# Embedding bags by counting: VectorE parts four table chunks instead of three, and ScalarE copies every upper part

## The reference, cut to what matters

```python
flat = tables.reshape(F_ * V_, E_)
emb = flat[ids + offs]                      # 512 x 32 x 20 x 64
mask = (jnp.arange(L_) < lengths[..., None]).astype(emb.dtype)
pooled = jnp.einsum('bfle,bfl->bfe', emb, mask)
return jnp.nan_to_num(pooled.reshape(Bq, F_ * E_))
```

## Time and profile before

| | |
|---|---|
| time, median of 3 runs | 1303.89 us (1300.76 to 1318.76) |
| the profiled execution's own time | 1306.5 us |
| its span | 1304.4 us |
| mean granted clock of TensorE | 0.934 |
| busy share of the span | PE 77%, DVE 71%, ACT 62%, POOL 55% |
| chain of work that ended last, by engine | PE 55%, ACT 18%, DVE 11%, another core or an unknown queue 8%, issue 7% |

### The profile page before, as it was taken

How to read it: one execution, slowest core, us unless ns; L and a number is a source line. 1 busy time by engine, 2 the same in 40 slices (tenths; PEclk the granted TensorE clock), 3 DMA queues, 4 the chain that set the end, 5 groups by cost and what they waited for, 6 DMA issues and landing times.

```text
span 1304.4 us, 28164 instructions
## 1 busy us (share of the span) xinstructions
PE 1002.7 (77%) x9391; PEld 835.3 (64%) x9391; DVE 929.9 (71%) x2543; ACT 811.9 (62%) x1198; POOL 721.5 (55%) x667
## 2 busy tenths in 40 slices
PE   3438887886887787778788777787878778879996
PEld 1226776765766666566666566675767666767876
DVE  9915757785977776767777677786777768768891
ACT  3525857674857575657475656675767666667881
POOL 3874656665665565645756646666666665652010
PEclk9958999998989988989989899998999989899998
DMA  4402322433333423224242424251515242413120
GB/s 176 168 10 56 79 73 64 120 99 96 105 102 100 122 79 114 84 63 129 79 120 77 123 60 128 72 157 43 149 52 156 65 127 74 124 35 106 45 66 6
DMA packets 67286, 120.72 MB, mean 93 GB/s; under 512 B 32329, under 2 KB 34131, under 8 KB 67208
## 3 DMA queue, kind: packets, MB, share of 16 engines
q1 hardware_dynamic: 45240, 99.89, 24.2%
q0 software_dynamic: 20768, 19.49, 7.8%
q10 hardware_dynamic: 1200, 0.62, 0.2%
HBM read 81.61 MB, written 4.75 MB: 66 GB/s over the span
## 4 chain that ended last, share of the span: by engine, by line
PE 55%; ACT 18%; DVE 11%; another core or an unknown queue 8%; issue 7%; DVEq 0%; DMA 0%
PE sums L575 30%; PE pairs L566 19%; ACT counts L508 10%; PE rest L594 5%; DVE onehot_j L792 4%; ACT rest L516 3%; ACT parts L525 2%; ACT parts L533 1%; DVE onehot_p L790 1%; ACT parts L529 1%; ACT parts L521 1%; DVE table L804 1%; DVE parts L810 1%; DVE rows L852 0%
## 5 line engine op out<-in xcount | busy, mean ns | idle before, releaser
L461 POOL DMA_INDIRECT rows<-tables,row_now x537 | 595.7, 1109 | 417.9 <-PE pairs L566 261.2
L575 PE MATMUL sums<-parts,counts 128*128 128x192 bf16 x7448 | 785.8, 255 | 0.8 <-issue 0.8
L508 ACT ACTIVATE counts<-pairs 128x588 int16<-128x588 f32 (+1 forms) x836 | 529.8, 649 | 392.1 <-PE pairs L566 255.4
L575 PEld LDWEIGHTS sums<-parts,counts 128*128 128x128 fp8e3 x7448 | 672.7, 102 | 51.6 <-issue 1.6
L566 PE MATMUL pairs<-onehot_j,onehot_p 128*128 128x294 bf16 x1634 | 366.5, 306 | 177.9 <-ACT counts L508 116.5
L792 DVE TENSOR_SCALAR onehot_j<-ramp,j_of,worth 128x296 bf16<-128x296 f16 x1596 | 470.1, 356 | 0.0
L790 DVE TENSOR_TENSOR onehot_p<-ramp,p_of 128x768 bf16<-128x768 f16 x266 | 146.6, 551 | 329.1 <-PE pairs L566 226.4
L566 PEld LDWEIGHTS pairs<-onehot_j,onehot_p 128*128 128x128 bf16 x1634 | 158.2, 101 | 263.8 <-issue 168.1
L471 POOL DMA_INDIRECT out_gathered<-gathered,place_now x52 | 59.7, 1147 | 99.0 <-DVE gathered L822 83.7
L525 ACT ACTIVATE parts<-rest 128x896 bf16<-128x896 f32 x76 | 69.6, 916 | 40.9 <-remote 24.7
L594 PE MATMUL rest<-table,minus_eye 128*128 128x448 bf16 x152 | 46.4, 388 | 51.4 <-ACT rest L516 33.7
(11 more groups left out here) (74 smaller groups left out, 238.0 us busy)
## 6 DMA issues: line engine op xcount, KB each, us to landing
table<-tables SPq DMA_DIRECT2D x133, 448.0 KB
rows<-zeros SPq DMA_DIRECT2D x52, 640.0 KB
rows<-tables,row_now POOLq DMA_INDIRECT x537
out_counted<-pooled SPq DMA_DIRECT2D x114, 21.0 KB
sorted_records<-records,rank POOLq DMA_INDIRECT x52
out_gathered<-gathered,place_now POOLq DMA_INDIRECT x52
rows<-lookup_ids SPq DMA_DIRECT2D x1, 774.0 KB, 7.9
rows<-lookup_lengths SPq DMA_DIRECT2D x1, 774.0 KB, 9.2
```

What stands on the lines that cost most here:

```text
L461: nc.gpsimd.indirect_dma_start(out=rows[:, k, l * E:(l + 1) * E], out_offset=None, in_=table_rows, in_offset=bass.IndirectOffsetOnAxis(ap= ...
L508: nc.scalar.activation(dst, src, ACT.Copy).then_inc(counts_saved, 1)
L575: last = nc.tensor.matmul(sums[h][:, k * PARTS * E:(k + 1) * PARTS * E], counts[h][:, j, :, k], parts[:, j].rearrange("p t e -> p (t e)"), ...
```

## The change

VectorE parts chunk 4 as well, so it has chunks 1, 3, 4 and 6, and PE's way is left with 0, 2 and 5. ACT copies the upper halves of all seven chunks (`HIGH_AT` has seven entries), and DVE's clamp (`cut_high`) and its semaphore are gone. `cut_rest` subtracts the upper halves of the words, read in the chunk itself with a stride of two bfloat16, and writes the remainder into a new buffer `remains` that holds two chunks, in place of the chunk. `save_cut_middle` and `cut_low` read that buffer. In a first use of a chunk PE waits for its upper part too. Slots and stages of most of this work are moved.

```diff
-PARTED_AT = {0: 9, 2: 16, 4: 24, 5: 29}
-HIGH_AT = {0: 7, 2: 15, 4: 21, 5: 28}
-PARTED_BY_VECTOR = {5: 1, 8: 3, 11: 6}
-MIDDLE_AT = {1: 14, 3: 23, 6: 32}
-BF16_MAX = 3.3895313892515355e38
+PARTED_AT = {0: 9, 2: 16, 5: 28}
+HIGH_AT = {0: 7, 1: 12, 2: 19, 3: 22, 4: 24, 5: 25, 6: 34}
+PARTED_BY_VECTOR = {5: 1, 7: 3, 9: 4, 11: 6}
+MIDDLE_AT = {1: 14, 3: 20, 4: 26, 6: 32}
...
+        remains = sb("remains", [P, 2, CE], F32)
...
+        def remains_of(c):
+            return remains[:, by_vector.index(c) % 2, :].rearrange("p (j e) -> p j e", e=E)
...
             def save_cut_middle(f, c):
                 act.wait_ge(rest_done, f * len(by_vector) + by_vector.index(c) + 1)
-                nc.scalar.activation(part_rows(1, c), table_rows_of(c), ACT.Copy).then_inc(cut_middle_saved, 1)
+                nc.scalar.activation(part_rows(1, c), remains_of(c), ACT.Copy).then_inc(cut_middle_saved, 1)
...
                             if h == 1 and q == 0:
+                                pe.wait_ge(high_saved, f * CHUNKS + (c + 1))
                                 if c in PARTED_AT:
                                     pe.wait_ge(low_saved, parted(f, c))
...
-            def cut_high(f, c):
-                dve.wait_ge(table_in[c], f * 16 + 16)
-                nc.vector.tensor_scalar(part_rows(0, c), table_rows_of(c), BF16_MAX, -BF16_MAX, ALU.min,
-                                        ALU.max).then_inc(high_done, 1)
             def cut_rest(f, c):
-                dve.wait_ge(high_done, f * len(by_vector) + by_vector.index(c) + 1)
-                nc.vector.tensor_tensor(table_rows_of(c), table_rows_of(c), part_rows(0, c),
-                                        ALU.subtract).then_inc(rest_done, 1)
+                dve.wait_ge(table_in[c], f * 16 + 16)
+                uppers = whole(c).bitcast(BF16).rearrange("p (j e y) -> p j e y", e=E, y=2)[:, :, :, 1]
+                nc.vector.tensor_tensor(remains_of(c), table_rows_of(c), uppers, ALU.subtract).then_inc(rest_done, 1)
             def cut_low(f, c):
                 dve.wait_ge(cut_middle_saved, f * len(by_vector) + by_vector.index(c) + 1)
-                nc.vector.tensor_tensor(part_rows(2, c), table_rows_of(c), part_rows(1, c),
+                nc.vector.tensor_tensor(part_rows(2, c), remains_of(c), part_rows(1, c),
                                         ALU.subtract).then_inc(parts_ready, 1)
...
                     onehots(f, h, c, i)
-                    if stage in PARTED_BY_VECTOR and i == 0:
-                        cut_high(f, PARTED_BY_VECTOR[stage])
-                    if stage in PARTED_BY_VECTOR and i == 2:
+                    if stage in PARTED_BY_VECTOR and i == 1:
                         cut_rest(f, PARTED_BY_VECTOR[stage])
                     if stage - 1 in PARTED_BY_VECTOR and i == 4:
                         cut_low(f, PARTED_BY_VECTOR[stage - 1])
```

More of the change, by code:

```diff
@@ L120, in build_embedding_bag @@
     assert LAST_BODY in (SLOTS, BUFFERS) and BUFFERS % 2 == 0 and BODIES > 1
+    assert sorted(HIGH_AT) == sorted(HIGH_AT, key=HIGH_AT.get) == list(range(CHUNKS))
     assert J % CHUNKS == 0 and GROUPS * GROUP >= HALF and PER_CHUNK % 2 == 0 and CHUNKS * PER_CHUNK == LAST
@@ L234, in build_embedding_bag @@
         table_in = [sem(f"table_in{c}") for c in range(CHUNKS)]
-        high_done = sem("high_done")
         rest_done = sem("rest_done")
@@ L793, in onehots, with cut_rest @@
                                         ALU.is_equal, ALU.mult).then_inc(onehots_ready, 1)
-            def cut_high(f, c):
+            def cut_rest(f, c):
                 dve.wait_ge(table_in[c], f * 16 + 16)
-                nc.vector.tensor_scalar(part_rows(0, c), table_rows_of(c), BF16_MAX, -BF16_MAX, ALU.min,
-                                        ALU.max).then_inc(high_done, 1)
-            def cut_rest(f, c):
-                dve.wait_ge(high_done, f * len(by_vector) + by_vector.index(c) + 1)
-                nc.vector.tensor_tensor(table_rows_of(c), table_rows_of(c), part_rows(0, c),
-                                        ALU.subtract).then_inc(rest_done, 1)
+                uppers = whole(c).bitcast(BF16).rearrange("p (j e y) -> p j e y", e=E, y=2)[:, :, :, 1]
+                nc.vector.tensor_tensor(remains_of(c), table_rows_of(c), uppers, ALU.subtract).then_inc(rest_done, 1)
             def cut_low(f, c):
                 dve.wait_ge(cut_middle_saved, f * len(by_vector) + by_vector.index(c) + 1)
-                nc.vector.tensor_tensor(part_rows(2, c), table_rows_of(c), part_rows(1, c),
+                nc.vector.tensor_tensor(part_rows(2, c), remains_of(c), part_rows(1, c),
                                         ALU.subtract).then_inc(parts_ready, 1)
```

## The result

In the first series the kernel before took 1314.94 us (median of five runs, the three shown and two new ones, 1300.76 to 1318.76) and the changed kernel 1293.44 us (1287.75 to 1308.06). The ratio is 0.987, with a 95% interval from 0.982 to 0.991: 1.3% faster, where 2.1% was forecast. The profiled execution of the changed kernel was the slowest of its five, 1308 us against 1288 to 1294, so its span is not compared with that of before; its slots are.

The account below looks back on a forecast made before the run. PE was taken as the bound, DVE right behind. Terms -1.95 - 0.6 + 0.6 + 0.4 = -1.55 us a field, over 18 fields 28 us: 1306.5 to 1278.5, less 2.6 for the median, 1276 us; range 1256 to 1308.

Parts of the forecast that it names:

- within 2%: Outcome class for the whole time, neither faster than 1278 us nor slower than 1330 us: chance 0.48.
- late results: PE results coming late in fields other than 17, costing 10 to 14 us a field; the prediction held them fixed.
- ACT's queue: One more ACT operation a field, lag in slots 16 to 26: +0.6 us, the middle of nothing to 1.2.
- the cuts beside the gathers: Two more long DVE cuts a field beside POOL's gathers: at most 2.2 us more of POOL's time, charged nothing.
- Chunk 4 leaves PE's way: Slots 25 and 26 become plain, 3.94 us to 1.99: -1.95 us a field, all on PE's path.
- Chunk 2's upper copy: It leaves slot 15, so the copy into PSUM comes sooner and slot 17's wait goes: -0.6 us a field.
- the 0.3 that chunk 5 was given either way: Chunk 5's upper copy leaves slot 28 and the group in 24 to 26 replaces it: nothing, between -0.3 and +0.3 us.
- DVE, +0.4: Four rests and lows replace three clamps, rests and lows: 0.32 us more DVE work, rounded up, all charged a field.
- the strided input at 1086 ns: DVE's rest subtracting strided bfloat16 into a separate output: assumed as long as the present rest, 1086 ns.
- The fourth rival: Cuts hold POOL's gathers 2.2 us a field and DVE waits for rows: 12 us more, 1316 us; chance 0.03.
- DVE in PE's place: Rival: DVE's work and slack limit the field, cutting the gain to some 0.5 us a field: 1295 us; chance 0.24.
- ACT blocked at cut middle parts: Rival: at slots 20, 26 and 32 ACT waits for DVE's rest, costing 4.4 us a field: 1355 us; chance 0.06.

Follow-up runs that it names:

- bursts: Kernel before and changed kernel, each with six bursts of 40 useless matmuls a field on PE: 1274.71 and 1269.91 us, 1.232 and 1.240 of the kernel before without them.
- e5: The kernel before, unchanged, run again for its profile under the later series' conditions: 1023.34 us.
- e8: The kernel before with upper copies of chunks 2, 4 and 5 moved to slots 20, 27 and 34, and PE's wait for them added: 1022.56 us, 0.998.
- e1: The changed kernel again, no edit, in the later series: 1046.13 us, 1.020 of the kernel before.
- e4: The changed kernel with upper copies of chunks 2 to 6 spread to slots 21, 23, 25, 34 and 36: 1046.13 us, 1.021 of the kernel before.
- e16: The changed kernel with chunk 4 back in PE's way and upper copies placed away from copies into PSUM: 1018.79 us, 0.995 of the kernel before.
- e17: e16 with cut middles of chunks 3 and 6 at slots 20 and 34, upper copies of 2 and 5 at 21 and 33: 1015.41 us, 0.992.
- e12: The kernel of e8 with chunk 3 in PE's way as well and upper copies in free slots: 1037.76 us, 1.014 of the kernel before.
- e7: The changed kernel without its 537 gathers and their lengths, DVE still adding up every tile: 1001.56 us, 0.977 of the kernel before.
- e11: The kernel before without its gathers and their lengths: 1003.48 us, 0.980 of the kernel before with them.
- e6: The changed kernel with its eight cuts a field as equally long one-input reductions, no remainders computed: 1007.95 us, 0.984 of the kernel before.
- e14: The kernel before with its six two-input cuts a field as equally long one-input reductions, no remainders computed: 1007.99 us, 0.985.
- e13: The changed kernel a third time, no edit, in the later series: 1047.60 us, 1.023 of the kernel before.
- e2: The kernel before with only chunk 4 moved from PE's way to DVE, clamp and in-place rest kept: 1048.57 us, 1.023.
- e15: The changed kernel with upper copies spread as in e4 and one-input cuts as in e6, no remainders computed: 1004.31 us, 0.981 of the kernel before.

## Why the prediction was right or wrong

*The direction and the condition.* The sign was right in the first series, 1.3% of the 2.1%, and wrong in every later one. The prediction's own chances put 0.48 on "within 2%" and 0.45 on more, and the measured ratio lies in the first while being clear of no change. The forecast of 1276 us also stood on a kernel before of 1303.89 us, whose median with two more runs is 1314.94. The sum was made for fields of 65 us, in which late results hold PE back. It named them and held them fixed, which the runs don't support as a property of the kernel: in every later series they are nearly absent, and the sign turns.

*The steps that failed.* Two, one for the size and one for the sign. The sum of the path was too large: -1.55 us a field was forecast, and undisturbed slots give -0.50, with and without bursts, so the prediction's 28 us would be 9. Its term for ACT's queue, +0.6, is too small in the medians of both conditions (+1.28 and +1.48). And the term for the cuts beside the gathers, put at nothing, costs 1.3 to 1.4 us a field where POOL has no slack, which turns the gain into a loss of 2%. In the first series that second term was nothing as forecast (DVE waits 4.3 us for rows, 5.3 before), so the shortfall there is of the first kind.

*Chunk 4 leaves PE's way, -1.95.* Right where it was read: in the first series slots 25 and 26 take 4.12 and 2.15 us in the medians, -1.97, and -2.00 in the means. Mis-sized as a property of an undisturbed field: 1.19 (3.35 to 2.16). The row that it was read from, a slot 25 of 2.38 us, came two slots after a slot 23 of 2.41 us with 1.17 us of idle time, so the field looked undisturbed and was not. The median slot 25 is 1.79 in e5 and 2.29 in the first series. The starts of slots 23 and 24 in the kernel before:

```profile
1202.06 0.41 PE L566 MATMUL pairs<-onehot_j,onehot_p 128*128 128x294 bf16 x2
...
1204.47 0.42 PE L566 MATMUL pairs<-onehot_j,onehot_p 128*128 128x294 bf16 x2 [1.17 <-issue]
```

*Chunk 2's upper copy, -0.6.* Right as a mechanism, measured -0.46 (-0.41 in the first series); e8 shows -0.63 when the copy is only moved. The change puts chunk 1's copy at slot 12, which takes a part back: slot 17 takes 1.64 us in e1, e4, e16 and e17, which have it there, and 1.47 in e8 and e12, which have none.

*ACT's queue, +0.6.* Mis-sized. Short count and slot 21 +0.91, slot 14 +0.13, slots 27 to 31 +0.24: 1.28. The bound of 1.2 for a lag of four slots was nearer than the middle, and the change in slots 27 to 31 lies within the 0.3 that chunk 5 was given either way. e4 gets 1.1 of it back by spreading the copies. In the first series the same slots give +1.48 by the medians, but +0.32 by the means.

*DVE, +0.4 and the strided input at 1086 ns.* The duration was right (1081 to 1084). The medians without this term sum to -1.19 - 0.46 + 1.28 - 0.12 = -0.49, against -0.50 measured: DVE's work costs nothing in the median field. In the mean field it is there: with no gathers the mean is 0.64 us over the median in the changed kernel (e7) and 0.26 in the kernel before (e11), and with one-input cuts 0.87 and 0.43 (e6 and e14). That is the 0.4 forecast, in slots 32 to 39 above all, and it leaves the change 0.14 us a field, the 2 us between e11 and e7.

*Two more cuts beside the gathers, nothing.* This was argued from POOL's idle time in one field, 30 of 70 us, and that idle time existed because PE was late. The fourth rival had the right mechanism for the later series, with a chance of 0.03 and a price of 2.2 us a field; measured, the cuts cost the changed kernel 38 to 40 us (e1 or e13 against e6) and the kernel before 15 (e14), a difference of 23 to 25 us or 1.3 to 1.4 a field over 18 fields. The price was of the right size and the chance was not, once POOL has no slack. As rows of the gathers show: 180 of 537 gathers overlap a cut in e1 and take 1424 ns, the others 1093; in e6, with one input, it is 1062 and 1106. The Trainium skill, "SBUF — State Buffer", section "Who interferes with whom", also says that a tensor reduction never contends with GpSimd on this chip; e6 and e14 agree, with cuts of 1069 to 1078 ns that hold no gather. The prediction took the gather of rows 9 as one blocked for coming second. By its own rows it came first, by 0.07 us, and was held all the same, as the 49 of e1 that began less than 0.2 us ahead of a cut were.

*The rivals.* DVE in PE's place (0.24) is seen in e2, and points the same way in e15, once the gathers are relieved. ACT blocked at cut middle parts (0.06): 26.6 us in 15 waits in e1, against 20.9 in 10 in e5 and 15.7 in 10 in e6, which has the same queue: 6 us more than before, and partly a sequel of the late rows. In the first series it is 8.3 us for 7.5.

*What is open.* Why the first series ran at 1300 us with late results is not known: the same program, the same 120.72 MB of transfers, and nearly the same work of DVE (busy for 930 and 920 us) and ACT (812 and 811). Nor is the 1.3% itself taken apart: medians say -0.8 us a field there (52.7 to 52.0), 14 us of the 17 to 21. The slots named above, with slot 34, sum to -1.03 by the medians and to -2.19 by the means, while the mean fields of the two executions differ by 0.11 only, since the late results fall into other slots. So which term ate the forecast gain in that series stays open; ACT's queue is the one that the medians name.

## What to carry to other kernels

Before work is moved to an engine, look at what runs beside it and is held by it, and read the slack of the engine that is held in the fastest condition that can be had: slack that exists since something else is late is not slack. An engine that only feeds transfers (POOL here) can be the bound at 79% busy, since its gaps between issues are work too; its wait for others (249 us in one profile, 29 in the other) tells whether it has slack, and its consumer's wait (DVE's for rows, 38 us in e1 and 4 in e6) whether the lack of it costs time. And take a price from the median of many repeats of a slot rather than from one field that looks clean.

## What the runs showed that was not expected

- The kernel before, unchanged, takes 1315 us in one series and 1023 us in all later ones, on five chips.
- A DVE instruction with two inputs in SBUF holds a POOL gather for up to its whole length (in e1 49 gathers of 1.99 us in the mean, beside cuts of 1.08), and one with one input of the same length doesn't. Whether it is held hangs on when it began: less than 0.2 us ahead of the cut or during it, yes; 0.2 us ahead or more, hardly (1049 ns). The second input is worth 113 ns in the mean of 537 gathers, 38 to 40 us in the time.
- Shorter fields were not paid out at all in e4 (1.1 us a field of path freed, time the same), and hardly with one-input cuts (0.1 in e15).
